# A mixture-of-experts kernel: an expert loop in rounds with one semaphore increment per engine, and POOL paced by small writes of zeros

## What is computed

```python
h = _L0_tok_ref(x, ...)                  # depthwise convolution, group norm, PReLU: (128, 125, 64) -> (128, 63, 64)
h = h + _L0_attn_ref(_layernorm(h), ...) # state-space scan along the 63 positions
h = h + _L0_ffn_ref(_layernorm(h), ...)

def _L0_ffn_ref(x, Wr, br, W1, b1, W2, b2):      # T = 8064 tokens of 64 channels, 64 experts
    logits = xf @ Wr + br
    topk_logits, topk_idx = jax.lax.top_k(logits, 2)
    gates = jax.nn.softmax(topk_logits, axis=1)
    combine = jnp.zeros((T, E)).at[jnp.arange(T)[:, None], topk_idx].add(gates)
    for e in range(E):
        h = jax.nn.relu(xf @ W1[e] + b1[e])      # 64 -> 128
        y = h @ W2[e] + b2[e]                    # 128 -> 64
        out = out + combine[:, e:e + 1] * y
    return out
```

## Time and profile before

| | |
|---|---|
| median of 3 runs | 859.83 us (858.7 to 861.21) |
| the profiled execution | 855.41 us |
| its span, first to last instruction | 853.5 us |
| POOL busy | 600.2 us, 70% |
| DVE busy | 565.8 us, 66% |
| PE busy | 511.2 us, 60% |
| mean granted TensorE clock | 0.826 of 2.4 GHz |

### The profile page before, as it was taken

How to read it: one execution, slowest core, us unless ns; L and a number is a source line. 1 busy time by engine, 2 the same in 40 slices (tenths; PEclk the granted TensorE clock), 3 DMA queues, 4 the chain that set the end, 5 groups by cost and what they waited for, 6 DMA issues and landing times.

```text
span 853.5 us, 9083 instructions
## 1 busy us (share of the span) xinstructions
PE 511.2 (60%) x2514; PEld 338.5 (40%) x2520; DVE 565.8 (66%) x1180; ACT 331.1 (39%) x622; POOL 600.2 (70%) x393
## 2 busy tenths in 40 slices
PE   4744245657568566556636767867677768786100
PEld 4733012222122222223323445756566657666100
DVE  1597899999999999997815763445444444332073
ACT  2159856556556655543311412323322332322000
POOL 5895779999999999991364454655555555564674
PEclk9969568797878789986756786999999998999655
DMA  7999950000000000000036013887877877831122
GB/s 247 383 180 123 74 3 0 0 0 0 0 1 0 0 0 0 0 0 0 20 84 161 15 67 110 229 222 211 235 225 209 241 214 208 224 90 47 23 73 62
DMA packets 106605, 84.96 MB, mean 100 GB/s; under 512 B 30464, under 2 KB 90240, under 8 KB 106560
## 3 DMA queue, kind: packets, MB, share of 16 engines
q1 hardware_dynamic: 79312, 54.76, 29.8%
q10 hardware_dynamic: 19184, 21.40, 8.0%
q0 software_dynamic: 8064, 8.27, 4.0%
HBM read 57.22 MB, written 33.49 MB: 106 GB/s over the span
## 4 chain that ended last, share of the span: by engine, by line
POOL 28%; PE 24%; DVE 16%; issue 14%; another core or an unknown queue 11%; ACT 4%; SPq 1%; POOLq 1%; DMA 0%; DVEq 0%; ACTq 0%
POOL x_w L577 14%; POOL w_ring L570 11%; PE ps L910 10%; PE ps L897 5%; POOL xt L650 3%; DVE x_w L1610 2%; DVE x_w L1620 2%; PE ps L675 2%; PE ps L739 1%; PE ps L886 1%; DVE mi L1515 1%; DVE lstat L1297 1%; PE ps L766 1%; PE ps L664 1%
## 5 line engine op out<-in xcount | busy, mean ns | idle before, releaser
L739 PE MATMUL ps<-x_w,ident 128*128 128x512 f32 x252 | 153.8, 770 | 100.7 <-POOL x_w L577 100.7
L629 POOL DMA_INDIRECT sorted_rows<-xp,slot_i x126 | 123.7, 981 | 116.4 <-DVE x_w L1620 35.2
L650 POOL DMA_INDIRECT xt<-expert_out,slot_i x126 | 123.3, 979 | 84.7 <-DVE x_w L1620 42.7
L570 POOL TENSOR_TENSOR w_ring<-xt,bc 128x2016 f32<-128x2016 f32 x32 | 143.4, 4483 | 13.4 <-DVE hh_ring L1426 7.3
L1426 DVE TENSOR_TENSOR_SCAN hh_ring<-ps,w_ring 128x1024 f32<-128x1024 f32 x64 | 147.5, 2305 | 0.1
L577 POOL TENSOR_TENSOR x_w<-hh_ring,bc 128x2016 f32<-128x2016 f32 (+1 forms) x32 | 141.1, 4411 | 1.2 <-PE ps L739 1.2
L739 PEld LDWEIGHTS ps<-x_w,ident 128*128 128x128 f32 x252 | 60.2, 249 | 197.0 <-POOL x_w L577 123.2
L1620 DVE COPY x_w<-ps 128x256 f32<-128x256 f32 x80 | 33.9, 424 | 108.0 <-remote 53.7
L1074 ACT ACTIVATE ps<-dt_t,a_exp 128x1024 f32<-128x1024 f32 x64 | 71.6, 1119 | 64.2 <-DVE hh_ring L1426 64.1
L1068 ACT ACTIVATE ps<-dt_t,a_exp 128x1024 f32<-128x1024 f32 x64 | 71.6, 1119 | 51.0 <-DVE w_ring L1405 51.0
L1165 ACT ACTIVATE x_w<-ps 128x256 f32<-128x256 f32 x80 | 30.8, 385 | 138.7 <-PE ps L886 57.6
(11 more groups left out here) (209 smaller groups left out, 887.9 us busy)
## 6 DMA issues: line engine op xcount, KB each, us to landing
dt_t<-packed SPq DMA_DIRECT2D x140, 96.5 KB
x_w<-packed SPq DMA_DIRECT2D x112, 96.5 KB
x_w<-sorted_rows ACTq DMA_DIRECT2D x40, 256.0 KB
expert_out<-x_w ACTq DMA_DIRECT2D x80, 128.0 KB
sorted_rows<-pad_rows SPq DMA_DIRECT2D x2, 3584.0 KB, 24.1
bc<-packed SPq DMA_DIRECT2D x68, 96.5 KB
packed<-in_L_ffn_W SPq DMA_DIRECT2D x3, 2048.0 KB, 42.0
x_w<-in_x SPq DMA_DIRECT2D x7, 448.0 KB, 8.7
```

Source lines behind the costliest of these rows:

```text
L570: pool.tensor_tensor(w_buf(k, 2), up3[:, bass.ds(c * DC, DC), 1:S].unsqueeze(1).broadcast_to([P, 2, DC, L]), vec_of(k, 2), ALU.mult).then_ ...
L629: pool.indirect_dma_start(out=sorted_rows[h], out_offset=bass.IndirectOffsetOnAxis(ap=slot_i[:, c, l:l + 1], axis=0), in_=xn[:, l, :], in_ ...
L650: pool.indirect_dma_start(out=y[:, l, :], out_offset=None, in_=expert_out[h], in_offset=bass.IndirectOffsetOnAxis(ap=slot_i[:, c, l:l + 1] ...
L739: ins = pe.matmul(ps[:, i, :], ident[:, :], src[:, i * BANK:(i + 1) * BANK], start=(k < 0), stop=(k == (N - 2 if last else N - 1)), skip_g ...
```

## The change

Three things change. First, the expert loop is written in rounds. In round k PE does `outputs(k - 4)`, `hidden(k - 2)` and `rows_T(k)`, ACT does `xT_copy(k)` and `relu_A(k - 2)`, DVE does `relu_B(k - 2)` and `y_copy(k - 4)`, and each engine makes one increment at the end of its round (`s_pstep`, `s_astep`, `s_dstep`) in place of one for every piece. ACT and DVE wait for PE's same round, PE waits for their rounds k - 2. `outputs` multiplies with 128 columns in place of 192, and its results lie in one PSUM bank, alternately in bank 6 and 7. Second, DVE makes fewer increments of `s_dve` in the routing and in `gates_at`: one behind a row of instructions in place of one for each. Third, the three tables of waits are gone, and `keep_pace(d)` writes zeros to a new scratch tile `beat` of 128 x 128 for every even d, with an increment of `s_pool` for which POOL waits before the next transfer.

```diff
+LAG_H, LATE = 2, 4
-OUT = 3 * C
+OUT = 2 * C
...
-GROUP_AT = {18: 3, 21: 4, 25: 5, 38: 6, 41: 7, 44: 8}
-STEP_AT = {d: (d - FIRST_STEP - LAG) * STEP0[-1] // 153 for d in range(FIRST_STEP + LAG + EVERY, FIRST_STEP + LAG + 154, EVERY)}
-BIAS_AT = {212 + 3 * q: q + 1 for q in range(CQ)}
...
+def dve_rounds(steps):
+    return steps + LATE - LAG_H
...
                 if n >= WRING:
-                    sp.wait_ge(s_yb, step_of(n - WRING) + 1)
+                    sp.wait_ge(s_dstep, dve_rounds(step_of(n - WRING) + 1))
...
             def keep_pace(d):
 
-                if d in GROUP_AT:
-                    pool.wait_ge(s_hot, GROUP_AT[d])
-                if d in STEP_AT:
-                    pool.wait_ge(s_yb, STEP_AT[d])
-                if d in BIAS_AT:
-                    pool.wait_ge(s_cbc, BIAS_AT[d])
+                if d % 2 == 0:
+                    ch.link(pool.memset(beat[:, :], 0.0))
...
-                        last = pe.matmul(ps[:, 6 + j, t * OUT:(t + 1) * OUT], hT_e[:, i % 2, t, j, :],
-                                         w_of(n)[:, t, 0:OUT], start=True, stop=True)
-                last.then_inc(s_yps, 1)
+                        last = pe.matmul(ps[:, 6 + i % 2, (2 * j + t) * OUT:(2 * j + t + 1) * OUT], hT_e[:, i % 2, t, j, :],
+                                         w_of(n)[:, t, HID + C - OUT:HID + C], start=True, stop=True)
+                return last
...
+            for k in range(STEP0[-1] + LATE):
+                if k >= LAG_H:
+                    pe.wait_ge(s_astep, k - LAG_H + 1)
+                if k >= LATE:
+                    pe.wait_ge(s_dstep, k - 2 * LAG_H + 1)
+                    last = outputs(k - LATE)
+                if LAG_H <= k < STEP0[-1] + LAG_H:
+                    last = hidden(k - LAG_H)
+                if k < STEP0[-1]:
+                    last = rows_T(k)
+                last.then_inc(s_pstep, 1)
...
+            for k in range(STEP0[-1] + LAG_H):
+                act.wait_ge(s_pstep, k + 1)
+                if k < STEP0[-1]:
+                    last = xT_copy(k)
+                if k >= LAG_H:
+                    last = relu_A(k - LAG_H)
+                last.then_inc(s_astep, 1)
+                if k < STEP0[-1]:
+                    next_rows(k)
+                if k > LATE:
+                    store(k - LATE - 1)
...
                 for l in range(v.start, v.stop):
-                    dve.max(mx[:, l, :], logits[:, l, :]).then_inc(s_dve, 1)
-                ch.at = ch.at + v.stop - v.start
-                dve.wait_ge(s_dve, ch.at)
+                    last = dve.max(mx[:, l, :], logits[:, l, :])
+                ch.link(last)
...
+            for k in range(LAG_H, STEP0[-1] + LATE):
+                dve.wait_ge(s_pstep, k + 1)
+                if k < STEP0[-1] + LAG_H:
+                    last = relu_B(k - LAG_H)
+                if k >= LATE:
+                    last = y_copy(k - LATE)
+                last.then_inc(s_dstep, 1)
```

More of the change, by code:

```diff
@@ L899, in hidden @@
                                          xT_e[t * C:(t + 1) * C, i % 2, j, :], start=True, stop=True)
-                last.then_inc(s_hid, 1)
+                return last
             def outputs(i):
[L904 to L907, removed]
                 for j, n in enumerate(pairs_of(i)):
                     for t in range(2):
-                        last = pe.matmul(ps[:, 6 + j, t * OUT:(t + 1) * OUT], hT_e[:, i % 2, t, j, :],
-                                         w_of(n)[:, t, 0:OUT], start=True, stop=True)
-                last.then_inc(s_yps, 1)
[L914 to L922, removed]
+                        last = pe.matmul(ps[:, 6 + i % 2, (2 * j + t) * OUT:(2 * j + t + 1) * OUT], hT_e[:, i % 2, t, j, :],
+                                         w_of(n)[:, t, HID + C - OUT:HID + C], start=True, stop=True)
+                return last
+            for k in range(STEP0[-1] + LATE):
[9 more added lines that the diff above has]
+                last.then_inc(s_pstep, 1)
             pe.wait_ge(s_b2, 32)
-            pe.wait_ge(s_yb, STEP0[-1])
+            pe.wait_ge(s_dstep, dve_rounds(STEP0[-1]))
             def bias_of(q):
@@ L1175, in relu_A @@
                                           bias=w_of(n)[:, 0, HID + C:WROW])
[L1176 removed]
+                return last
             def store(i):
                 q, m = in_share(pairs_of(i)[0]), len(pairs_of(i))
[L1181 removed]
+                act.wait_ge(s_dstep, dve_rounds(i + 1))
                 rows = expert_out[share_at(STEP0, i)].rearrange("(u p t) d -> u p t d", p=P, t=2 * UNIT)
@@ L1201, in _ @@
                 rows_of_unit(v)
[L1202 to L1214, removed]
+            for k in range(STEP0[-1] + LAG_H):
[9 more added lines that the diff above has]
+                    store(k - LATE - 1)
+            for i in range(STEP0[-1] + LAG_H - LATE - 1, STEP0[-1]):
+                store(i)
             for q in range(CQ):
@@ L1457, in positions_of @@
                 for l in range(a, z):
-                    dve.bn_stats(lstat[:, l, :], hg[:, l, :]).then_inc(s_dve, 1)
-                ch.at = ch.at + z - a
+                    last = dve.bn_stats(lstat[:, l, :], hg[:, l, :])
+                last.then_inc(s_dve, 1)
+                ch.at = ch.at + 1
             def variance_of(c):
@@ L1465, in variance_of @@
                 even, odd = lstat[:, span, 1], lstat[:, span, 4]
-                dve.tensor_tensor(lsm[:, 0, span], even, odd, ALU.add).then_inc(s_dve, 1)
-                dve.tensor_tensor(lsm[:, 2, span], lstat[:, span, 2], lstat[:, span, 5], ALU.add).then_inc(s_dve, 1)
-                ch.at = ch.at + 2
+                dve.tensor_tensor(lsm[:, 0, span], even, odd, ALU.add)
+                dve.tensor_tensor(lsm[:, 2, span], lstat[:, span, 2], lstat[:, span, 5], ALU.add)
                 ch.link(dve.tensor_tensor(lsm[:, 1, span], even, odd, ALU.subtract))
@@ L1510, in choose @@
                 for l in range(v.start, v.stop):
-                    dve.max(mx[:, l, :], logits[:, l, :]).then_inc(s_dve, 1)
-                ch.at = ch.at + v.stop - v.start
-                dve.wait_ge(s_dve, ch.at)
+                    last = dve.max(mx[:, l, :], logits[:, l, :])
+                ch.link(last)
                 for l in range(v.start, v.stop):
-                    dve.max_index(mi[:, l, :], mx[:, l, :], logits[:, l, :]).then_inc(s_dve, 1)
-                ch.at = ch.at + v.stop - v.start
-                dve.wait_ge(s_dve, ch.at)
+                    last = dve.max_index(mi[:, l, :], mx[:, l, :], logits[:, l, :])
+                ch.link(last)
                 ch.link(dve.tensor_copy(top[:, 2:4, v], mi[:, v, 0:2].rearrange("p l c -> p c l")))
@@ L1611, in relu_B @@
                                              w_of(n)[:, 1, HID + C:WROW], 0.0, ALU.add, ALU.max)
-                last.then_inc(s_reluB, 1)
+                return last
             def y_copy(i):
@@ L1628, in gates_at @@
                 for k in range(2):
-                    dve.tensor_scalar(comb[k][:, l, :], iota_e[:, :], top[:, 2 + k, l:l + 1], gates[k][:, l:l + 1],
-                                      ALU.is_equal, ALU.mult).then_inc(s_dve, 1)
-                ch.at = ch.at + 2
+                    last = dve.tensor_scalar(comb[k][:, l, :], iota_e[:, :], top[:, 2 + k, l:l + 1], gates[k][:, l:l + 1],
+                                             ALU.is_equal, ALU.mult)
+                if l % 8 == 7 or l + 1 == L:
+                    last.then_inc(s_dve, 1)
+                    ch.at = ch.at + 1
             def both_gates(q):
```

47 lines of the change are left out of this document (11 added, 36 removed).

## The result

The changed kernel takes **957.0 us** (955.42 to 957.91, 4 runs) against 859.27 us (855.6 to 861.21, 4 runs): ratio 1.1147, 95% interval [1.1112, 1.1182], 11.5% slower where 3.8% faster was forecast. Its span is 955.7 us.

The account below looks back on a forecast made before the run. POOL's sequence of 252 transfers was taken as the bound, its runs delaying other engines' increments. Start 417.65 + 0.26, 125 periods of 3.14, 2.84 and 7.7 give 821.0 us of span; with 1.9 and 4.4 added, 827 us, range 797 to 870.

Parts of the forecast that it names:

- the law: POOL's back-to-back transfers: other engines' increments wait for a gap or the backlog's end, 1.42 to 1.46 us for each transfer.
- the period of zeros and two transfers: POOL's new sequence: one set of zeros and two transfers repeats every 3.14 us, the zeros' own increment being held up.
- The lower bound: Low end of POOL's period: zeros' increment not held, yet 2.84 us needed for two transfers; 783.5 us span, 790 us.
- the prediction's sum: POOL's whole sequence: 417.65 + 0.26, 125 periods of 3.14, 2.84 and 7.7 give 821.0 us of span, 827 us median.
- The price of a late post: Expert loop: a post comes at most 0.6 us late in each period's last part, priced at 0.1 us a round.
- the signs of its being wrong: POOL's trace: period above 3.4 us, a gap of some us for stores or row numbers, or 2 us stalls following its pairs.
- The round of 2.6 us: Expert loop: each of the 39 rounds from 618 us on takes 2.6 us, where 3.15 would still cost nothing.
- (1): POOL's zeros run only after the transfers' backlog: period 3.34 us, 852 us, 0.9% faster; chance 0.22.
- (2): POOL's switch between zeros and transfer costs 0.73 us each time: period 3.87 us, 918 us, 6.8% slower; chance 0.13.
- (3): Expert loop stays the bound, rounds taking 3.6 us, say from a lower granted clock: 844 us; chance 0.08.
- (4): Stalls have another cause than runs of transfers, so zeros relieve nothing and a loop step keeps 3.2 us: 868 us; chance 0.07.
- The slower side's 0.18: Whole kernel: chance 0.18 of being slower by over 0.3%, from (2), most of (4), and periods above 3.41 us.

Follow-up runs that it names:

- the long zeros: The changed kernel with its tile of zeros 128 x 512 in place of 128 x 128: 824.95 us, ratio 0.9641 against the kernel before.

## Why the prediction was wrong, step by step

**The bound was right, the law in part.** Increments are held up while POOL issues transfers back to back, and the last of them is released when 1.42 to 1.46 us for each transfer are over: the release at 634.69 of the changed kernel and that at 2.89 us in each pair of the long zeros are the law of the earlier trace rows in two new places. But that a post "gets through only in a gap, or when the backlog is gone", and that only the first 2 us are free of it, does not hold in a long series: in that of 568.92 they came on time up to 574.37 and 1.1 us late at 577.64, and three more got through in its midst.

**The step that failed is the period of zeros and two transfers.** I put the zeros' own increment under the law of the others ("if it obeys the law"), which made 3.14 us. It measured 2.75. POOL's own increment comes without delay, and with it the zeros take 0.50 us from the end of one transfer to the start of the next (427.94 to 428.44), 0.20 us more than lie between two transfers without them.

**The lower bound was wrong in kind, and this is what cost the sign.** "The increment is not held but the backlog still needs 2.84 us for two, so 2.84" takes the backlog for something that slows POOL. The rows already said otherwise: POOL issues every 1.27 us while each transfer leaves 1.42 us. With the increment free, the period was to be worked out as 2 x 1.27 + 0.20 with what lies around it, which is below 2.84, and the result is then not a faster kernel but one in which no hole opens that could let the others on. At its lower bound of 2.84 us a pair the prediction's sum gives 790 us; the kernel with zeros of 128x256, with 2.85 us, took 927. The sign turns on the short side too, between 2.96 us a pair (888 us) and 3.02 (1.51 us a transfer, 846 us, ratio 0.9872). I had looked for its turn only on the long side, at 3.40.

**The price of a late post was wrong with it.** "A post is late by at most 0.6 us", 0.1 us a round, holds only where each period ends in a hole. In the changed kernel an increment was up to 18.8 us late (PE ends at 805.67, ACT and DVE start at 824.44), the loop fell behind, and POOL stood 142.3 us for its stores, which the prediction had named among the signs of its being wrong. By the sum and the measured period, 417.9 + 125 x 2.75 + 2.84 + 7.7 = 772 us of span would have been enough if nothing else held POOL; 955.7 was measured.

**The sum was right for its own period.** With 3.07 us of period, the long zeros' kernel, it gives 417.9 + 125 x 3.07 + 2.84 + 7.7 = 812 us of span; 821.0 was measured, with one wait of 5.2 us for stored results that I had not foreseen, a start 1.0 us later, and a mean of 1.57 us in the last 46 gathers. The median, 825 us, lies 2 us from the 827 forecast for a kernel that this one was not.

**The round of 2.6 us** was too long: 1.91 where nothing is held up, and one for each hole, 3.07, where holes pace it. The size of a round without holding up did not decide the sign. That the loop's gain is hidden held: with the tables it is worth nothing.

**The rivals.** (1) and (2), a longer period, are out: the zeros do not wait for the backlog, and the switch from zeros to a transfer is 0.28 us, not 0.73. Mechanism (1) leant on the rule cited there from the Trainium skill, "GPSIMD Engine Reference", Instruction dispatch, that a core of GpSimd goes on to the next instruction when its own share of the last is done. The trace shows the zeros at 427.93, at the recorded end of the transfer before, and ended at 428.16, so no part of them lay behind the backlog; it does not contradict the rule, but speaks for it that the backlog is not work that these cores still have to do. (3), the loop as the bound at 3.6 us a round, is out as put: where POOL is silent a round takes 1.91 us at a granted clock of 0.92. (4), another cause for the stalls, is out: the width of the zeros alone moves the time from 957 to 825 us. The slower side's 0.18 held the sign, but for none of its reasons.

**What stays open** is why 1.48 us a transfer, above the 1.42 to 1.46 measured for a backlog, still is not enough. With 2.89 us to the release, the hole of a 2.96 us period is 0.07 us, and I take it that spread in the backlog closes it often; that was argued, not shown. In the 128x384 kernel that took 887.55 us a round takes some 4.9 us there (ACT's L1151 at 544.27 and, 15 rounds on, at 617.81), neither one a period nor a standstill. Open are also what lets single increments through in the midst of a series, what the serial work is, and what changes the chip's condition between groups.

## What to carry to other kernels

A fixed pause in place of a wait is a bet on a number: here the kernel is faster than before with a mean time of an indirect transfer of 1.51 to 1.59 us, best at 1.54, and slower at 1.48 and less and at 1.75. At 1.37 it lost 11.5% against waits for other engines, which stop POOL when the others are late; a fixed pause doesn't. When a cost isn't in the rows, work out what the mechanism does at each side of its threshold, and not only what the sum gives there: the lower end of a cost can be the bad end. And try such a number at two or three sizes: 128, 384, 512 and 1024 columns give 957, 888, 825 and 870 us.

## What the runs showed of the hardware

The holding up comes and goes. The same kernel with 128x384 took 801.86 us in one group and 887.55 us in another, and the kernel before 759.36 and 858.27 us. It does not go by the chip alone: the group with 759.36 us and an earlier one with 856.39 us ran on the same chip, number 10. In the condition without holding up no engine waits for "remote" in the three kernels' traces, POOL's sends take as long as with it (979 ns beside 974 in the same kernel), and the version that is 3.6% faster with it was not timed there. The order of kernels turns: 128x256 for each is 3.2% faster than before with the holding up and 9.4% slower without it, because the kernel before gains by its absence and this one, bound by POOL, doesn't (830.18 and 829.78 us). With the holding up the transfers' own data are not late: in the changed kernel's first series of 32, the first transfer's packets begin 1.75 us after its issue and the last one's 1.58 us. What is late is the increments of other engines; POOL's own are not: within the three series from 568.92 to 840.4 us each set of zeros but the first of a series is followed by its transfer after 0.27 or 0.28 us.
